# Key and query projections in the loop: both parts of the input in one 512-column matmul, halves summed by VectorE

## The reference, cut to what matters

```python
x = x + (x @ W.T + per-sequence low-rank adapter)         # layer 0
x = x + einsum('bct,bcd->bdt', x, w1[idx1])               # layer 1, one 64x64 matrix per sequence; result called x1
x = x + attention(x, cond_1, Wq, Wk, Wv, Wo)              # layer 2, 16 heads of 32, causal, 64 keys
x = x + einsum('bct,bcd->bdt', x, w3[idx3])               # layer 3
```

## Time and profile before

| | |
|---|---|
| time, median of 3 runs | 608.24 us (607.91 to 608.48) |
| time of the profiled execution | 608.18 us |
| its span | 606.4 us |
| TensorE busy | 600.0 us, 99% of the span |
| VectorE busy | 392.6 us, 65% |
| ScalarE busy | 225.4 us, 37% |
| GpSimd busy | 110.5 us, 18% |
| granted TensorE clock | 1.00 (full, 2.4 GHz) |

### The profile page before, as it was taken

The page is one execution under the profiler, slowest core; times in us unless marked ns, Lnnn a source line. Parts: engine busy times, 40 slices in busy tenths (PEclk is TensorE's granted clock), DMA queues, the critical chain, the costliest instruction groups (busy, mean ns, idle before and its releaser), DMA issues.

```text
span 606.4 us, 21505 instructions
## 1 busy us (share of the span) xinstructions
PE 600.0 (99%) x8524; PEld 519.6 (86%) x8524; DVE 392.6 (65%) x573; ACT 225.4 (37%) x434; POOL 110.5 (18%) x101
## 2 busy tenths in 40 slices
PE   9999999999999999999999999999999999999998
PEld 8898989798898988889798898978889898888885
DVE  4699865766657576564866657576564766646374
ACT  4555352343424244251443514244252433413222
POOL 2013030402104040130402104040120403103030
PEclk9999999999999999999999999999999999999999
DMA  8862322231412323222231413322222231310312
GB/s 292 170 136 65 83 63 75 75 75 62 96 39 88 85 65 70 72 65 74 76 83 52 96 40 88 84 68 68 72 68 70 77 92 43 77 62 3 71 41 105
DMA packets 65272, 48.29 MB, mean 80 GB/s; under 512 B 16922, under 2 KB 51738, under 8 KB 65242
## 3 DMA queue, kind: packets, MB, share of 16 engines
q1 hardware_dynamic: 60090, 42.63, 26.7%
q10 hardware_dynamic: 5152, 5.24, 3.0%
HBM read 30.54 MB, written 17.30 MB: 79 GB/s over the span
## 4 chain that ended last, share of the span: by engine, by line
PE 99%; issue 1%; ACT 0%; DVE 0%; DVEq 0%
PE banks L653 10%; PE banks L658 10%; PE banks L654 10%; PE banks L681 5%; PE banks L754 5%; PE banks L755 5%; PE banks L683 5%; PE banks L685 5%; PE banks L593 5%; PE banks L595 5%; PE banks L597 5%; PE banks L761 5%; PE banks L708 5%; PE banks L700 4%; PE banks L724 4%; PE banks L620 3%
## 5 line engine op out<-in xcount | busy, mean ns | idle before, releaser
L653 PE MATMUL banks<-x1T_hi,w_hi 128*128 128x256 f32 x512 | 130.0, 286 | 0.0
L654 PE MATMUL banks<-x1T_hi,w_lo 128*128 128x256 f32 x512 | 128.4, 283 | 0.0
L653 PEld LDWEIGHTS banks<-x1T_hi,w_hi 128*128 128x128 f32 x512 | 96.8, 189 | 0.7 <-ACT x1T_hi L926 0.4
L654 PEld LDWEIGHTS banks<-x1T_hi,w_lo 128*128 128x128 f32 x512 | 96.9, 189 | 0.0
L1431 POOL TENSOR_TENSOR w_own<-w_in,own 128x128 f32<-128x128 f32 x32 | 15.3, 479 | 381.5 <-PE banks L620 283.0
L658 PE MATMUL banks<-x1T_lo,w_hi 128*128 128x256 f32 x512 | 82.4, 283 | 0.0
L1449 POOL TENSOR_TENSOR probs<-probs,row_max 128x1024 f32<-128x1024 f32 x32 | 61.0, 1907 | 91.5 <-DVE row_max L1224 91.5
L658 PEld LDWEIGHTS banks<-x1T_lo,w_hi 128*128 128x128 f32 x512 | 70.2, 189 | 0.2
L1210 DVE TENSOR_TENSOR qkT<-banks,beta 128x512 f32<-128x512 f32 x32 | 22.1, 691 | 60.4 <-PE banks L658 60.4
L926 ACT ACTIVATE attnT_hi<-banks 128x512 fp32r<-128x512 f32 (+1 forms) x32 | 17.1, 581 | 117.8 <-PE banks L724 117.5
L1228 DVE TENSOR_REDUCE row_sum<-probs 128x16 f32<-128x1024 f32 x32 | 39.0, 1219 | 24.1 <-ACT probs L1008 24.1
(11 more groups left out here) (138 smaller groups left out, 1047.3 us busy)
## 6 DMA issues: line engine op xcount, KB each, us to landing
x_rows<-x_in SPq DMA_DIRECT2D x64, 128.0 KB, 2.4
x_kept<-x_rows SPq DMA_DIRECT2D x16, 512.0 KB, 3.6
x_in<-in_x_dram SPq DMA_DIRECT2D x60, 128.0 KB, 2.8
out_dram<-x_y SPq DMA_DIRECT2D x15, 512.0 KB, 2.8
b_sel<-b_parts SPq DMA_DIRECT2D x180, 32.0 KB, 1.7
w_in<-in_L_cond_weights_dram SPq DMA_DIRECT2D x128, 16.0 KB
probsT<-in_L_cond_W_dram ACTq DMA_DIRECT2D x1, 1024.0 KB, 6.1
probs<-in_L_cond_Wk_dram ACTq DMA_DIRECT2D x1, 1024.0 KB, 5.3
```

Source lines behind the costliest of these rows:

```text
L653: nc.tensor.matmul(out_ap, w_hi[:, w, c, cols], x1T_hi[:, c, :], start=(c == 0), stop=False)
L654: nc.tensor.matmul(out_ap, w_lo[:, w, c, cols], x1T_hi[:, c, :], start=False, stop=False)
```

## The change

In the loop alone (steps 1 to 12), x1T_hi and x1T_lo become two halves of one tile, x1T_parts, laid side by side for each chunk c, so that one matmul can take 512 moving columns: the 256 tokens of the high part and the 256 of the low part. For each output chunk m, `project_parts` runs four pairs: w_hi x (high and low part, 512 columns), and w_lo x high part (256 columns, accumulated on the first half). The first half of the bank then holds hi*hi + lo*hi, the second half hi*lo. Every chunk m has a bank of its own: keys in MIX[0], MIX[1], SC[0], SC[1], queries in OUT[0], MIX[0], SC[2], SC[3]. VectorE sums the two halves with a `tensor_reduce` over a strided view (`sum_parts`); for queries a multiplication by beta in SBUF follows, behind a semaphore of its own. ScalarE copies no keys in the loop any more. The unrolled steps keep their way; there the counters k_mm and q_mm are only counted per chunk.

```diff
+K_OF = (MIX[0], MIX[1], SC[0], SC[1])
+Q_OF = (Q[0], Q[1], SC[2], SC[3])
-        x1T_hi = sb("x1T_hi", [P, NC, PT], F32R)
-        x1T_lo = sb("x1T_lo", [P, NC, PT], F32R)
+        x1T_parts = sb("x1T_parts", [P, NC, 2, PT], F32R)
+        x1T_hi = x1T_parts[:, :, 0, :]
+        x1T_lo = x1T_parts[:, :, 1, :]
...
+            def project_parts(w, to, m):
+                cols = slice(m * P, (m + 1) * P)
+                for c in range(NC):
+                    nc.tensor.matmul(bank[to], w_hi[:, w, c, cols], x1T_parts[:, c].rearrange("p a n -> p (a n)"),
+                                     start=(c == 0), stop=False)
+                    last = nc.tensor.matmul(bank[to][:, 0:PT], w_lo[:, w, c, cols], x1T_hi[:, c, :],
+                                            start=False, stop=(c == NC - 1))
+                return last
+
+            def keys_by_banks(i):
+                for m in range(NC):
+                    if m == 0:
+                        pe.wait_ge(x1_copied, SEQT * (i - 1) + 1)
+                    elif m == 1:
+                        pe.wait_ge(x1_copied, SEQT * i)
+                    elif m == 2:
+                        pT_copied(i - 1, 1)
+                    project_parts(WK, K_OF[m], m).then_inc(k_mm, 1)
+
+            def queries_by_banks(i):
+                for m in range(NC):
+                    if m == 1:
+                        pe.wait_ge(k_copied[0], i + 1)
+                    elif m == 2:
+                        pT_copied(i - 1, HG)
+                    elif m == 3:
+                        layer3_ready(i - 2)
+                    project_parts(WQ, Q_OF[m], m).then_inc(q_mm, 1)
...
             def scores(i):
-                for mm, k_copied in enumerate((k_copied_act, k_copied_dve)):
-                    pe.wait_ge(k_copied, i + 1)
-                    pe.wait_ge(q_scaled, 2 * i + mm + 1)
+                if not parted(i):
+                    pe.wait_ge(k_copied[1], i + 1)
+                    pe.wait_ge(q_scaled, 2 * i + 2)
...
+                if not parted(i):                      # TensorE, in step(i)
+                    pe.wait_ge(x1_split, TILES * (i + 2))
+                    keys_by_banks(i + 1)
+                    queries_by_banks(i + 1)
+                    attend()
+
+                    pe.wait_ge(q_scaled, 2 * i + 3)
+                    pe.sem_inc(queries_scaled, 1)
+                    layer3(i - 1)
+                    scores(i + 1)
+                    return
...
+            def sum_parts(dst, b):                     # VectorE
+                return nc.vector.tensor_reduce(dst, bank[b].rearrange("p (a n) -> p n a", a=2), AX.X, ALU.add)
+
+            def sum_k(i, half_of):
+                for m in (2 * half_of, 2 * half_of + 1):
+                    dve.wait_ge(k_mm, NC * i + m + 1)
+                    last = sum_parts(kT[:, m, :], K_OF[m])
+                last.then_inc(k_copied[half_of], 1)
+
+            def sum_q(i, half_of):
+                for m in (2 * half_of, 2 * half_of + 1):
+                    dve.wait_ge(q_mm, NC * i + m + 1)
+                    sum_parts(qT[:, m, :], Q_OF[m]).then_inc(q_summed, 1)
+                    dve.wait_ge(q_summed, NC * (i - 2) + m + 1)
+                    last = nc.vector.tensor_tensor(
+                        qT[:, m, :].rearrange("p (q s) -> p q s", s=S), qT[:, m, :].rearrange("p (q s) -> p q s", s=S),
+                        beta[:, bass.ds(i * PSEQ, PSEQ)].unsqueeze(2).to_broadcast([P, PSEQ, S]), ALU.mult)
+                last.then_inc(q_scaled, 1)
...
+                if not parted(i):                      # VectorE, in step(i), after x_lo(i + 2)
+                    sum_k(i + 1, 0)
                 if prev and after(i, 3):
                     turn_x(i + 3)
-                if prev:
-                    copy_k(i + 1)
-                scale_q(i + 1, range(1))
                 if not parted(i):
-                    scale_q(i + 1, range(1, 2))
-                if prev and parted(i):
-                    copy_y(i - 1)
+                    sum_k(i + 1, 1)
+                    for n in range(2):
+                        sum_q(i + 1, n)
```

More of the change, by code:

```diff
@@ L245, in cond_resid_kernel @@
         x1_split = sem("x1_split")
-        k_copied_act = sem("k_copied_act")
-        k_copied_dve = sem("k_copied_dve")
+        k_copied = [sem(f"k_copied{n}") for n in range(2)]
+        q_summed = sem("q_summed")
         q_scaled = sem("q_scaled")
@@ L663, in key_part @@
                 last = project_T(WK, MIX, m, split=TILES * (i + 1) if m == 0 else None)
[L664 to L665 removed]
+                last.then_inc(k_mm, 1)
             def query_part(m, split=None):
                 last = project_T(WQ, Q, m, split)
[L669 to L670 removed]
+                last.then_inc(q_mm, 1)
+            def project_parts(w, to, m):
[24 more added lines that the diff above has]
+                    project_parts(WQ, Q_OF[m], m).then_inc(q_mm, 1)
             def values(i, t, x0_of=None):
@@ L689, in scores @@
             def scores(i):
-                for mm, k_copied in enumerate((k_copied_act, k_copied_dve)):
-                    pe.wait_ge(k_copied, i + 1)
-                    pe.wait_ge(q_scaled, 2 * i + mm + 1)
+                if not parted(i):
+                    pe.wait_ge(k_copied[1], i + 1)
+                    pe.wait_ge(q_scaled, 2 * i + 2)
+                for mm in range(2):
+                    if parted(i):
+                        pe.wait_ge(k_copied[mm], i + 1)
+                        pe.wait_ge(q_scaled, 2 * i + mm + 1)
                     for t in range(TILES):
@@ L819, in step @@
                     if m == 2:
-                        pe.wait_ge(k_copied_act, i + 2)
-                    if prev and m == (1 if parted(i) else 3):
-                        pe.wait_ge(k_copied_dve, i + 2)
+                        pe.wait_ge(k_copied[0], i + 2)
+                    if prev and m == 1:
+                        pe.wait_ge(k_copied[1], i + 2)
                         pT_copied(i, HG)
@@ L825, in step @@
                     query_part(m)
-                    if m == (1 if parted(i) else 3):
+                    if m == 1:
                         if not prev:
-                            pe.wait_ge(k_copied_dve, 2)
+                            pe.wait_ge(k_copied[1], 2)
                             pT_copied(0, HG)
                             pe.wait_ge(xa_summed, 2)
-                        elif parted(i):
+                        else:
                             layer3(i - 1)
                         attend()
[L834 to L837, removed]
                 if not prev:
                     pe.wait_ge(part_split, len(PARTS_V) + len(PARTS_O))
-                elif parted(i):
+                else:
                     pe.wait_ge(y_copied_act, i)
@@ L902, in _ @@
                 if m == 2:
-                    pe.wait_ge(k_copied_act, 1)
+                    pe.wait_ge(k_copied[0], 1)
                 query_part(m)
@@ L998, in copy_k @@
             def copy_k(i):
-                act.wait_ge(k_mm, 2 * i + 1)
-                copy(kT[:, 0:2, :], bank[MIX[0]].rearrange("p (m n) -> p m n", n=PT)).then_inc(k_copied_act, 1)
+                act.wait_ge(k_mm, NC * i + 2)
+                copy(kT[:, 0:2, :], bank[MIX[0]].rearrange("p (m n) -> p m n", n=PT)).then_inc(k_copied[0], 1)
             def copy_v(i, t):
@@ L1055, in step @@
                     x_hi(i + 2)
-                if prev:
+                if prev and parted(i):
                     copy_k(i + 1)
-                if prev and parted(i):
                     copy_y(i - 1)
@@ L1203, in copy_k @@
             def copy_k(i):
-                dve.wait_ge(k_mm, 2 * (i + 1))
-                copy(kT[:, 2:4, :], bank[MIX[1]].rearrange("p (m n) -> p m n", n=PT)).then_inc(k_copied_dve, 1)
+                dve.wait_ge(k_mm, NC * (i + 1))
+                copy(kT[:, 2:4, :], bank[MIX[1]].rearrange("p (m n) -> p m n", n=PT)).then_inc(k_copied[1], 1)
+            def sum_parts(dst, b):
[14 more added lines that the diff above has]
+                last.then_inc(q_scaled, 1)
             def scale_q(i, halves=range(2)):
                 for n in halves:
-                    dve.wait_ge(q_mm, 2 * i + n + 1)
+                    dve.wait_ge(q_mm, NC * i + 2 * n + 2)
                     nc.vector.tensor_tensor(
@@ L1289, in step @@
                     x_lo(i + 2)
+                if not parted(i):
+                    sum_k(i + 1, 0)
                 if prev and after(i, 3):
                     turn_x(i + 3)
-                if prev:
-                    copy_k(i + 1)
-                scale_q(i + 1, range(1))
                 if not parted(i):
-                    scale_q(i + 1, range(1, 2))
-                if prev and parted(i):
-                    copy_y(i - 1)
+                    sum_k(i + 1, 1)
+                    for n in range(2):
+                        sum_q(i + 1, n)
+                else:
+                    if prev:
+                        copy_k(i + 1)
```

(3 more changed lines are left out.)

## The result

The changed kernel took 609.95 us (median of 22 runs, 606.48 to 611.44) against 607.93 for the kernel before (22 runs, 607.46 to 608.71). The ratio is 1.0024, 95% interval 1.0013 to 1.0035. The forecast was 603.1. The 22 times form two groups: six with a granted clock of 0.999 or 1.00 at 606.5 to 608.6 us, sixteen with one of 0.994 to 0.997 at 609.4 to 611.4.

What follows compares the result with a forecast made beforehand. TensorE, busy 99% of the span, was taken as the bound. Fewer fixed terms save 5.1 us, added waits and VectorE work cost nothing: 608.2 - 5.1 = 603.1 us, range 602.2 to 603.8, upper end stretched to 605.

Steps and rivals of the forecast that it cites:

- the price of a 512-column matmul beside one of 256: Keys and queries: 0.2 us extra per 512-column matmul would add 6.4 us to the stretch; the prediction took nothing.
- The columns stay, the fixed terms go: 12 x 0.43 = 5.1 us.: Keys and queries: 96 matmuls become 64, dropping 32 fixed terms of 13.3 ns, 0.43 us per step, over 12 steps.
- The unrolled steps keep their way, so their time stays: Steps outside the loop: no term for them; the sum counts only the loop's 12 steps, 608.2 - 5.1 us.
- The loop's first pass.: Start of the loop: part of a spread of a few tenths of a microsecond, 602.2 to 603.8 us.
- Waits on TensorE cost nothing.: Keys start only after x1's low part, with 1.7 us of cover; other waits are covered or satisfied, price nothing.
- The reduction takes 0.69, the product 0.43, and 1.2 us of cover remain.: VectorE before the scores: last product at 323.17, needed by TensorE at 324.40, so the new path costs nothing.
- the slower rival: VectorE between x_lo and scores: strided reductions at 1.12 us make TensorE wait 2.1 us per step, 628 us; 8%.
- the penalty that the prediction carried over: VectorE's PSUM reads in the reduction: a penalty per access to a new 8-byte line; weighed, but 0.69 us taken.
- The chances.: Whole kernel: faster by over 0.2% 0.86, within 0.2% 0.06, slower 0.08.

Runs made afterwards that it cites:

- 64 spread fillers: Changed kernel plus 64 semaphore increments nobody waits for, one behind each of 64 512-column matmuls in step 13: 603.41 us, on another chip 605.72 us.
- its two variants: The kernel before with only semaphore increments nobody waits for added: 192 in rows in steps 13 and 14, 632.09 us; 64 spread singly in step 13, 608.49 us.

## Why the prediction was wrong, step by step

Two steps failed: the time of the code that was not touched was taken as unchanged, and the price of a 512-column matmul beside one of 256 was put at nothing extra. By the traces the tail lost 3.9 us, the loop took 434.74 us where the forecast needs 436.65 - 5.1 = 431.55, 3.2 us more, and the stretch ahead of the loop gave 0.2 back: the 6.9 us between forecast and result.

- *The columns stay, the fixed terms go: 12 x 0.43 = 5.1 us.* The mechanism was right, the size was not. With the tail's gap out of the way (64 spread fillers) the change is worth 608.11 - 603.41 = 4.7 us at its shorter time and 608.19 - 605.72 = 2.5 us at its longer one. The term that was mis-sized is the price of a 512-column matmul beside one of 256. The prediction saw that no row had this neighbourhood, took its bounds from 0.2 us down to nothing, and chose nothing, because a single change of width in the earlier trace rows (transposes to the first 256) cost nothing visible. In the trace it costs 6.7 ns per pair, 32 x 6.7 = 0.21 us per step, half of the gain of 0.43. Two digits of microseconds can't show such a cost on one instruction; only the sum over many can.
- *The unrolled steps keep their way, so their time stays* (not written, but built into the sum, which stops at 12 steps). This failed, and it turned a gain into a loss. Of the 609.95 - 603.1 = 6.9 us, the tail has 3.9: 2.10 of waiting for code, 0.3 around it, and 1.5 at the lower clock behind it. Nothing of their work changed; their place did. The one row that could have warned stood in the trace of before: 0.68 us of "issue" in the first pass's scores, at 106.84, which the kernel before already paid at a block's end (shown in the next item).
- *The loop's first pass.* Forecast as a spread of a few tenths. Its wait for code is 1.17 us in the changed kernel, 0.68 in the kernel before (first line the changed one's):

```profile
106.78 1.17 issue
...
106.84 0.68 issue
```

  In the twelve traces the gap there was between 0.8 and 1.4 us, start to start. The kernel before and its two variants, which are alike up to that place, had 0.9, 1.1 and 1.3, so the difference is mostly chance.
- *Waits on TensorE cost nothing.* Right. Inside the loop TensorE's only idle time is "issue", 1.5 us in all (0.9 before); none has VectorE or ScalarE as its releaser.
- *The reduction takes 0.69, the product 0.43, and 1.2 us of cover remain.* Right, and the slower rival with them falls. VectorE's timeline, changed kernel, beside the earlier trace rows:

```profile
312.70 1.28 DVE L1253 TENSOR_REDUCE qkT<-banks 128x256 f32<-128x512 f32 x2
313.90 2.06 DVE L1190 STREAM_TRANSPOSE xT<-x_in 128x1024 f32<-128x1024 f32 x1
...
321.30 0.69 DVE L1253 TENSOR_REDUCE qkT<-banks 128x256 f32<-128x512 f32 x1 [0.26 <-PE banks L682]
322.02 0.43 DVE L1267 TENSOR_TENSOR qkT<-qkT,beta 128x256 f32<-128x256 f32 x1
```

  The last product ends at 322.45, the scores start at 323.69: 1.24 us. The step of 1 KB in PSUM cost VectorE nothing that shows: 0.69 us, as the copy of as many elements in the earlier trace rows. The note of the Trainium skill on lines (SBUF — State Buffer, on "cachelines"), which the prediction weighed against the earlier trace rows, says of PSUM that non-contiguous access slows matmuls down; the penalty that the prediction carried over from it to a VectorE read did not come.
- *The chances.* 8% stood on slower, for a mechanism that did not occur. The one that did was on no list.

## What to carry to other kernels

A change of a TensorE program's length is also a change of where its code blocks end, and this can cost or give time in code that was not touched, here 3.9 us. When a small gain doesn't arrive, compare the untouched stretches first, look for "issue" gaps, and count instructions to them modulo 256; then shift the code with hidden fillers before judging the change itself. And where a forecast rests on a few nanoseconds per instruction, the neighbourhood must be in the trace too, not only the instruction.

## What the runs showed of the hardware that was not expected

- The request for the 256 instructions that begin in the last attend left up to 3.4 us ahead of and up to 2.6 us behind the execution of the block end before them (the table), by what TensorE was doing there; over all traces a packet took 0.9 to 1.8 us.
- In the traces the gap of 2.10 us on TensorE, at a granted clock of 1.00, was followed by a stretch at 1.2 GHz that cost 1.5 us more, and so was the one of 2.75; those of 2.41 and 2.56 were not (the 512-column matmuls behind them are 0.23 apart). 16 of the changed kernel's 22 runs had a mean granted clock below 0.999.
- Matmuls of 256 columns alone cost 120.0 ns and of 512 alone 226.7; in turn a pair costs 353.4, in groups of four 350.5, in groups of eight 348.8 per pair, against 346.7 for the sum.
- Semaphore increments on TensorE's queue cost nothing that shows when single between matmuls of 512 columns (64 of them: 608.49 against 608.19, interval through 1), and about 67 ns each in rows of eight (4.3 us for 64).
- The same program with widths in turn and 64 spread fillers took 602.9 to 603.7 us in four runs and 605.6 to 606.1 in the other six. What chooses stays open.
